# Who copies the last state of four scans: VectorE or GpSimd

## The chip, the cores and the metric

One core of one Trainium2 chip runs the whole program in one launch. The metric is device time in microseconds (us), the median of several runs. Five engines have their own instruction streams and meet only through semaphores: TensorE (PE, with its weight loads as PEld), VectorE (DVE), ScalarE (ACT), GpSimd (POOL) and SyncE (SP), which here only issues transfers.

## The reference, cut to what matters

The program is a chain of four layers on x of shape (2, 4096, 512). The first, a state-space (Mamba) layer, is where the change lies:

```python
proj = x @ in_proj_w                     # hidden and gate, 1024 channels each
hs = silu(causal_conv4(hidden) + conv_b)
dt, Bm, Cm = split(hs @ x_proj_w)        # 128, 16, 16; each rms-normed
dt = softplus(dt @ dt_proj_w + dt_proj_b)
dA  = exp(dt[..., None] * A)             # A: 1024 x 16
dBu = (dt * u)[..., None] * Bm[:, :, None, :]
s = dA_t * s + dBu_t                     # the scan over time, for each channel and each of 16 states
y = sum_n s_n * C_n                      # C of this time step
out = ((y + u * D) * silu(gate)) @ out_proj_w
```

Three further layers (a mixed linear layer, a linear attention, a spline layer) follow in another function of the program, which the change does not touch.

## The kernel before

`mamba_block` works in 16 periods: 8 chunks of 512 time steps for each of 2 sequences, the two in turn (`periods`). A period has U = 32 units, numbered k. A unit is one group of 128 channels with 4 of the 16 states. What happens to unit k:

- PE, `b_product(k)` (L737): dt·u times B for the four states into the PSUM tile BU. There is one BU, so it waits until the four scans of unit k-1 are done (`scan_done`).
- ACT (L501): exp(dt·A) into the slot s[k % 4], four instructions.
- DVE (L651): four scans of 512 steps over s[k % 4] and BU, in place in s, each started from a column of `state`. Each adds one to `scan_done`.
- DVE, `piece(k)`: a share of the work for the next period or the previous output, placed by hand: `Y_AT`, `HID_AT`, `RES_AT`, `MIN_AT`, `MAX_AT`, `DTU_AT` and single numbers say which unit carries what. Units 14 to 21 carry one convolution each (L536, L540, three L544 with drains between). Unit 19 has `dt_floor` (L574) directly behind the third L544. Unit 3 has `add_res` (L590) and `dt_max` (L579). Unit 4 has `ln_apply` (two L528) and, directly behind, `dt_times_u` (L584). Units 13, 22 and 30 have L579 and then L584, which waits for it. Unit 10 has statistics (L518 to L523, with drains) and `add_res`, unit 11 `ln_apply` and `add_res`, unit 27 `ssm_norm` (L562, two L566), units 1, 9 and 25 `y_out` (L600, reads PSUM), units 0, 12 and 29 `dt_floor`. Units 5, 7, 8, 23, 24, 28 and 31 carry nothing.
- DVE (L656): a tensor_reduce over an axis of length 1, that is a copy, of the last column of the four scans into `state[:, b, k, :]` (128x4), where the scans of the same sequence's next chunk start. It adds one to `state_saved`.
- POOL (L335): waits for `state_saved`, then multiplies s by C (the tile Cb) in place, in two instructions of 128x1024. It must come behind the copy, since it overwrites the column. Each adds one to `z_ready`.
- PE, `y_sum` (L754): sums the products of a pair of units into PSUM; at an even k it needs the first half of unit k-1. It then frees the slot for ACT (`sum_done`).

POOL also has three small powers a period (L300, L304), each ahead of the product of units 2, 10 and 26, and four products of 128x512 (L310), behind the products of units 28, 29, 30 and 0. `dve.sem_inc` is an instruction of its own; in `add_res` one stands behind a wait for the result of L590 (L593, L594). PE's order in a unit is: wait for the scans of unit k-1, `b_product(k)`, and then `y_sum` and projections in an order fixed by k.

The inner part of the DVE body and of the POOL body, and all that calls them:

Of the kernel before, what the change touches and what calls it, by code (L numbers as in the profile page):

```python
# [9 lines left out]
ALU = mybir.AluOpType  # L10
ACT = mybir.ActivationFunctionType
AX = mybir.AxisListType

P = 128
T = 512
# [6 lines left out]
def wait(eng, sem, value):  # L22

    if not isinstance(value, int) or value > 0:
        eng.wait_ge(sem, value)
# [33 lines left out]
def mamba_block(nc, x, in_w, chan, xproj_w, dt_w, out_w, eye, tokmask, x1):  # L59
# [9 lines left out]
    U = G * NQ  # L69
# [4 lines left out]
    SLOTS = 4  # L74
# [6 lines left out]
    with ctx:  # L81
        def sb(name, shape, dt=F32):
            return ctx.enter_context(nc.sbuf_tensor(name, shape, dt))
# [4 lines left out]
        def sem(name):  # L88
            return ctx.enter_context(nc.semaphore(name))
# [7 lines left out]
        skip_w = sb("skip_w", [P, G, 64])  # L97
        mask = sb("mask", [P, 32])
        minus_half = sb("minus_half", [P, NT * 3])
        xt = sb("xt", [P, 2, HID])  # L100
        dts = sb("dts", [P, 2, T])
        xnT = sb("xnT", [P, KB, T])
# [8 lines left out]
        s = [sb(f"s{i}", [P, 4, T]) for i in range(SLOTS)]  # L111
        Cb = [sb(f"Cb{i}", [P, 4 * T]) for i in range(2)]
        state = sb("state", [P, BATCH, U, 4])
# [29 lines left out]
        spread_ready = sem("spread_ready")  # L143
        dbu_ready, da_ready, scan_done, state_saved = (
            sem("dbu_ready"), sem("da_ready"), sem("scan_done"), sem("state_saved"))
        z_ready, sum_done, y_ready = sem("z_ready"), sem("sum_done"), sem("y_ready")
        res_loaded = [sem(f"res_loaded{i}") for i in range(2)]
        x1_ready = sem("x1_ready")
# [44 lines left out]
        def periods(eng, body):  # L193

            for b in range(BATCH):
                body(0, b, b, b == 0, False)
            with eng.Fori(1, NI - 1) as i:
                for b in range(BATCH):
                    body(i, b, i * BATCH + b, False, False)
            for b in range(BATCH):  # L200
                body(NI - 1, b, (NI - 1) * BATCH + b, False, b == BATCH - 1)
# [89 lines left out]
        @block.gpsimd  # L291
        def _(pool):
            nc.gpsimd.memset(minus_half[:], -0.5)
            nc.gpsimd.memset(state[:], 0.0)
            nc.gpsimd.memset(hist[:], 0.0)
            pool.drain().then_inc(consts_ready, 1)

            def ln_power(c_next, half):
                wait(pool, stats_ready, 2 * c_next + half + 1)
                nc.gpsimd.tensor_tensor(rstd[:], ve[:], minus_half[:, 0:2], ALU.pow).then_inc(rstd_ready, 1)  # L300

            def ssm_power(c_next):
                wait(pool, ssq_ready, c_next + 1)
                nc.gpsimd.tensor_tensor(rssm.rearrange("p j n -> p (j n)"), ssq.rearrange("p j n -> p (j n)"),  # L304
                                        minus_half[:], ALU.pow).then_inc(rssm_ready, 1)

            def spread_b(c_next, nq):
                pool.wait_ge(ssm_ready, c_next + 1)
                lo = RANK + 4 * nq
                nc.gpsimd.tensor_tensor(spread[:, nq], mask[:].unsqueeze(1).unsqueeze(3).to_broadcast([P, TB, 32, 4]),  # L310
                                        ssm[:, :, lo:lo + 4].unsqueeze(2).to_broadcast([P, TB, 32, 4]),
                                        ALU.mult).then_inc(spread_ready, 1)

            ln_power(0, 0)
            ln_power(0, 1)
            ssm_power(0)
            pool.wait_ge(small_loaded, 48)
            for nq in range(NQ):
                spread_b(0, nq)

            def body(i, b, c, first, last):
                for k in range(U):
                    if k == 2 and not last:
                        ln_power(c + 1, 0)
                    if k == 10 and not last:
                        ln_power(c + 1, 1)
                    if k == K_SUMS and not last:
                        ssm_power(c + 1)
                    q = k // 2
                    if k % 2 == 0:  # L330
                        wait(pool, c_loaded[q % 2], 16 * (c * (U // 4) + (q % (U // 2)) // 2 + 1))
                    wait(pool, state_saved, c * U + k + 1)
                    for part in range(2):
                        pair = s[k % SLOTS][:, 2 * part:2 * part + 2, :].rearrange("p n t -> p (n t)")
                        nc.gpsimd.tensor_tensor(pair, pair, Cb[q % 2][:, 2 * part * T:2 * part * T + 2 * T],  # L335
                                                ALU.mult).then_inc(z_ready, 1)
                    if k == 0 and not first:
                        wait(pool, dbu_ready, c * U)
                        spread_b(c, 3)
                    if k in (28, 29, 30) and not last:  # L340
                        nq = k - 28
                        wait(pool, dbu_ready, c * U + 26 + 2 * nq)
                        spread_b(c + 1, nq)

            periods(pool, body)

        @block.scalar
# [166 lines left out]
        def _(dve):  # L514
# [10 lines left out]
            def ln_apply(c_next, half):  # L525
                wait(dve, rstd_ready, 2 * c_next + half + 1)
                for j in range(2):
                    last_ = nc.vector.tensor_scalar(xt[:, j, :], xt[:, j, :], mv[:, j, 0:1], rstd[:, j:j + 1],  # L528
                                                    ALU.subtract, ALU.mult)
                last_.then_inc(xn_ready, 1)  # L530
# [65 lines left out]
            def y_out(p, c, slot):  # L596
                wait(dve, gate_ready, 2 * c + p // 2 + 1)
                dve.wait_ge(sum_done, c * U + UP * (p + 1))
                for r in range(2):
                    nc.vector.tensor_tensor(u[slot][:, 2 * p + r, :], Y[r][:], gate[:, 2 * p + r, :], ALU.mult  # L600
                                            ).then_inc(y_ready, 1)
# [13 lines left out]
            def body(i, b, c, first, last):  # L615
                def piece(k):

                    if k == 1 and not first:
                        y_out(3, c - 1, 1 - b)
                    if k in Y_AT:  # L620
                        y_out(Y_AT[k], c, b)
                    if not last:
                        if k in (2, 10):
                            ln_stats(c + 1, 0 if k == 2 else 1)
                        if k in (4, 11):
                            ln_apply(c + 1, 0 if k == 4 else 1)
                        if k - 1 in HID_AT:
                            conv(steady, HID_AT[k - 1], c, 1 - b, 1 - b)
                        if k == K_SUMS:
                            ssm_sums(c + 1)  # L630
                        if k == K_NORM:
                            ssm_norm(steady, c, c + 1)
                    if k in RES_AT:
                        if first:
                            dve.drain().then_inc(steady.taken["dve"], 1)
                        else:
                            add_res(steady, RES_AT[k], c, c - 1)
                    if k in MIN_AT and not (last and MIN_AT[k] == 0):
                        dt_floor(steady, MIN_AT[k], c)
                    if k in MAX_AT and not (last and MAX_AT[k] == 0):  # L640
                        p = MAX_AT[k]
                        dt_max(p, PAIRS * c + (p if p else PAIRS))
                    if k in DTU_AT and not (last and DTU_AT[k] == 0):
                        p = DTU_AT[k]
                        dt_times_u(p, PAIRS * c + (p if p else PAIRS), c if p else c + 1, b if p else 1 - b)

                for k in range(U):
                    wait(dve, dbu_ready, c * U + k + 1)
                    for n in range(4):
                        wait(dve, da_ready, 4 * (c * U + k) + n + 1)  # L650
                        nc.vector.tensor_tensor_scan(s[k % SLOTS][:, n, :], s[k % SLOTS][:, n, :], BU[:, n::4],  # L651
                                                     state[:, b, k, n:n + 1], ALU.mult, ALU.add
                                                     ).then_inc(scan_done, 1)
                    piece(k)
                    wait(dve, scan_done, 4 * (c * U + k + 1))
                    nc.vector.tensor_reduce(state[:, b, k, :], s[k % SLOTS][:, :, T - 1:T], AX.X, ALU.max  # L656
                                            ).then_inc(state_saved, 1)

            periods(dve, body)
            y_out(3, NCH - 1, 1)  # L660
# [1139 lines left out]
```

## Time and the profile before

| what | value |
|---|---|
| median of 3 runs | 5924.46 us (5921.22 to 5928.32) |
| profiled execution, its time | 5923.98 us |
| profiled execution, its span | 5922.2 us |
| state-space layer, first to last L656 | 128.4 to 3790.5 us |
| busy in the span | PE 86%, DVE 83%, POOL 55%, PEld 51%, ACT 44% |

### The profile page before, as it was taken

To read this page: it belongs to the slowest core of one execution; us is meant where nothing else is said; L and a number is where in the kernel's file an instruction comes from. 1 tells how busy PE (TensorE), PEld (TensorE's weight loads), DVE (VectorE), ACT (ScalarE), POOL (GpSimd) and SP (SyncE) were. 2 spreads that over 40 slices of the span, in tenths; PEclk is the share of its full clock that TensorE was granted. 3 is DMA by queue.
4 is the path that set the end of the run, shared out by engine and by line. 5 is a ranking of instruction groups with operands and counts; after the bars stand their busy time and mean duration, and the time that the engine had idled before them with its cause. 6 is when DMAs were issued, how large, how long until landed. Compare 5 with 4: busy or idle time off the path is not lost. (4 is left out here: it accounts for less than half of the span.)

```text
span 5922.2 us, 110904 instructions
## 1 busy us (share of the span) xinstructions
PE 5088.3 (86%) x41157; PEld 3047.7 (51%) x41157; DVE 4925.7 (83%) x7468; ACT 2610.0 (44%) x4180; POOL 3231.1 (55%) x1675
## 2 busy tenths in 40 slices
PE   6899999999999999999999998668888888888822
PEld 3444444444444444444444444246666777777722
DVE  3888988888888889889888888568888888888888
ACT  3655655655556556556556555212222222222200
POOL 1676676676766766766766767423333333333323
PEclk9999999999999999999999999879999998899855
DMA  2221222222222222212222222220000000000034
GB/s 84 76 101 65 100 99 74 94 87 79 101 81 85 101 79 86 95 72 101 90 76 101 85 81 94 91 86 25 20 22 22 20 23 20 24 20 20 18 111 138
DMA packets 139954, 421.27 MB, mean 71 GB/s; under 512 B 38368, under 2 KB 39904, under 8 KB 106592
## 3 DMA queue, kind: packets, MB, share of 16 engines
q1 hardware_dynamic: 136672, 411.75, 19.8%
q8 instruction: 268, 4.39, 0.3%
q10 hardware_dynamic: 2816, 3.51, 0.2%
q14 instruction: 198, 1.62, 0.1%
HBM read 361.99 MB, written 53.22 MB: 70 GB/s over the span
## 5 line engine op out<-in xcount | busy, mean ns | idle before, releaser
L335 POOL TENSOR_TENSOR s<-s,Cb 128x1024 f32<-128x1024 f32 x1024 | 2393.7, 2359 | 1083.8 <-DVE state L656 1073.0
L651 DVE TENSOR_TENSOR_SCAN s<-s,state,BU 128x512 f32<-128x512 f32 x2048 | 2452.7, 1260 | 425.4 <-PE BU L737 391.5
L501 ACT ACTIVATE s<-dt,ch 128x512 f32<-128x512 f32 x2048 | 1305.6, 712 | 778.6 <-PE Y L754 777.1
L754 PE MATMUL Y<-s,ident 64*64 64x512 f32 x8192 | 1011.8, 609 | 76.2 <-POOL s L335 75.3
L683 PE MATMUL PJ<-xnT,w_in 128*128 128x512 f32 x2048 | 946.9, 606 | 9.1 <-ACT dtuT L367 5.7
L737 PEld LDWEIGHTS BU<-spread,dtuT 32*128 32x128 f32 x16384 | 512.7, 189 | 528.4 <-DVE s L651 403.0
L737 PE MATMUL BU<-spread,dtuT 32*128 32x128 f32 x16384 | 611.2, 286 | 145.5 <-DVE s L651 140.8
L683 PEld LDWEIGHTS PJ<-xnT,w_in 128*128 128x128 f32 x2048 | 370.1, 190 | 479.0 <-issue 424.2
L754 PEld LDWEIGHTS Y<-s,ident 64*64 64x64 f32 x8192 | 279.3, 134 | 571.5 <-issue 533.8
L728 PE MATMUL PJ<-w_out,u 128*128 128x512 f32 x1024 | 472.8, 606 | 8.2 <-ACT xnT L371 6.7
L1110 POOL TENSOR_TENSOR x1t<-x1t,bias_b 128x512 f32<-128x512 f32 x64 | 81.1, 1267 | 525.8 <-DVE xa L1282 525.8
L1463 PE MATMUL bank<-w_high_o,aTs 128*128 128x512 f32 x512 | 214.2, 485 | 125.7 <-DVEq L1385 125.7
L728 PEld LDWEIGHTS PJ<-w_out,u 128*128 128x128 f32 x1024 | 185.1, 190 | 243.3 <-issue 225.9
L544 DVE SCALAR_TENSOR_TENSOR u<-hid,ch,u 128x512 f32<-128x512 f32 x384 | 287.5, 749 | 19.1
L1104 POOL TENSOR_TENSOR r_t<-x,x3n 128x512 f32<-128x512 f32 x64 | 82.6, 1290 | 344.8 <-DVE x3n L1282 344.8
L694 PE MATMUL PJ<-w_xp,u 128*128 128x160 f32 x1024 | 253.0, 404 | 9.6 <-issue 6.5
L694 PEld LDWEIGHTS PJ<-w_xp,u 128*128 128x128 f32 x1024 | 243.1, 329 | 27.2 <-issue 20.8
L1463 PE MATMUL bank<-w_high_f,xaT 128*128 128x512 f32 x512 | 198.7, 452 | 12.5 <-DVE xaT L1287 12.5
L1225 ACT ACTIVATE junk<-bank 128x512 f32<-128x512 f32 x64 | 38.2, 598 | 380.4 <-PE bank L1535 380.4
L1463 PEld LDWEIGHTS bank<-w_high_o,aTs 128*128 128x128 f32 x512 | 119.8, 234 | 163.8 <-issue 135.2
L1161 ACT COPY qk_all<-bank 128x512 f32<-128x512 f32 x128 | 75.1, 587 | 227.1 <-PE bank L1463 227.1
L367 ACT COPY dtuT<-PJ 128x512 f32<-128x512 f32 x128 | 68.8, 587 | 231.3 <-PE PJ L723 231.3
(218 smaller groups left out, 7634.8 us busy)
## 6 DMA issues: line engine op xcount, KB each, us to landing
Cb<-bc SPq DMA_DIRECT2D x256, 1024.0 KB, 4.9
res<-in_x SPq DMA_DIRECT2D x64, 256.0 KB, 4.9
x<-res SPq DMA_DIRECT2D x64, 256.0 KB, 5.2
x1t<-x SPq DMA_DIRECT2D x64, 256.0 KB, 2.6
out<-r_t SPq DMA_DIRECT2D x64, 256.0 KB, 2.0
xt<-in_x SPq DMA_DIRECT2D x31, 512.0 KB, 5.5
x_all<-out SPq DMA_DIRECT2D x16, 512.0 KB, 4.2
scm<-out SPq DMA_DIRECT2D x16, 512.0 KB, 4.6
```

Source lines behind the costliest of these rows:

```text
L335: nc.gpsimd.tensor_tensor(pair, pair, Cb[q % 2][:, 2 * part * T:2 * part * T + 2 * T], ALU.mult).then_inc(z_ready, 1)
L501: nc.scalar.activation(s[k % SLOTS][:, n, :], dt[p % 2][:, gi, :], ACT.Exp, scale=ch[:, 2 * p + gi, 7 + 4 * nq + n:8 + 4 * nq + n]).then_i ...
L544: last_ = nc.vector.scalar_tensor_tensor(out, h_[:, tap:tap + T], ch[:, m, tap:tap + 1], out, ALU.mult, ALU.add)
L651: nc.vector.tensor_tensor_scan(s[k % SLOTS][:, n, :], s[k % SLOTS][:, n, :], BU[:, n::4], state[:, b, k, n:n + 1], ALU.mult, ALU.add).then ...
L683: last_ = nc.tensor.matmul(bank[:], w_in[:, kb, lo:lo + P], xnT[:, kb, :], start=(kb == 0), stop=(kb == KB - 1))
L694: last_ = nc.tensor.matmul(bank[:, tb % 2 * SP_:(tb % 2 + 1) * SP_], by_block(u[slot][:, g, :])[:, tb], w_xp[:, g, :], start=(g == 0), sto ...
L728: last_ = nc.tensor.matmul(bank[:], u[slot][:, g, j * P:(j + 1) * P], w_out[:, g, :], start=(g == 0), stop=(g == G - 1))
L737: last_ = nc.tensor.matmul(BU[:, i * T:(i + 1) * T].rearrange("p (t b n) -> p b t n", b=TB, n=4)[:, tb], dtuT[rows, gi, tb, :], spread[row ...
L754: last_ = nc.tensor.matmul(Y[r][y_rows(r, gi), :], ident[rows, rows], s[(k_even + gi) % SLOTS][rows, n, :], start=False, stop=(n == 3 and ...
L1104: nc.gpsimd.tensor_tensor(r_t[s_][:], x3[s_][:], x3n[s_][:], ALU.add).then_inc(S["r_ready"], 1)
L1110: nc.gpsimd.tensor_tensor(x1t[s_][:], x1t[s_][:], bias_b[:], ALU.add).then_inc(S["x1b_ready"], 1)
L1463: last_ = nc.tensor.matmul(b_[:], src[part][:, k, :], wt, start=(k == 0 and i == 0), stop=(k == KB - 1 and i == 2))
```

## The change

The copy leaves DVE. POOL waits for the four scans itself, multiplies the last column by a tile of ones into `state`, then waits for `pieces_done` and for its own copy, and multiplies by C. DVE's stream gets a bare `sem_inc(pieces_done)` behind the piece in place of the wait and the copy.

```diff
+        ones4 = sb("ones4", [P, 4])
...
+        pieces_done = sem("pieces_done")
...
             nc.gpsimd.memset(minus_half[:], -0.5)
+            nc.gpsimd.memset(ones4[:], 1.0)
...
                     if k % 2 == 0:
                         wait(pool, c_loaded[q % 2], 16 * (c * (U // 4) + (q % (U // 2)) // 2 + 1))
+                    pool.wait_ge(scan_done, 4 * (c * U + k + 1))
+                    last_col = s[k % SLOTS][:, :, T - 1]
+                    nc.gpsimd.tensor_tensor(state[:, b, k, :], last_col, ones4[:], ALU.mult).then_inc(state_saved, 1)
+                    wait(pool, pieces_done, c * U + k + 1)
                     wait(pool, state_saved, c * U + k + 1)
...
                     piece(k)
-                    wait(dve, scan_done, 4 * (c * U + k + 1))
-                    nc.vector.tensor_reduce(state[:, b, k, :], s[k % SLOTS][:, :, T - 1:T], AX.X, ALU.max
-                                            ).then_inc(state_saved, 1)
+                    dve.sem_inc(pieces_done, 1)
```

## Rows read from the trace of the kernel before

**Rows 1.** The page, section 2: busy tenths of PE in 40 slices, and DVE.

```profile
PE   6899999999999999999999998668888888888822
DVE  3888988888888889889888888568888888888888
```

**Rows 2.** Waits: who waited for whom, us in total, times, longest.

```profile
POOL s L335 <- DVE state L656: 1073.0, 462, 32.2
```

**Rows 3.** Timeline of DVE, units 3 to 6 of one period: start, duration, instructions, idle before.

```profile
1992.73 1.52 DVE L579 TENSOR_TENSOR dt<-dt,dts 128x1024 f32<-128x1024 f32 x1 [0.23 <-DVE res L590]
...
1998.95 0.97 DVE L528 TENSOR_SCALAR xt<-xt,mv,rstd 128x512 f32<-128x512 f32 x2
1999.84 1.21 DVE L584 TENSOR_TENSOR dts<-dt,u 128x1024 f32<-128x1024 f32 x1
2000.98 0.14 DVE L656 TENSOR_REDUCE state<-s 128x4 f32<-128x4 f32 x1
2001.05 4.78 DVE L651 TENSOR_TENSOR_SCAN s<-s,state,BU 128x512 f32<-128x512 f32 x4
2005.86 0.16 DVE L656 TENSOR_REDUCE state<-s 128x4 f32<-128x4 f32 x1
2007.21 1.28 DVE L651 TENSOR_TENSOR_SCAN s<-s,state,BU 128x512 f32<-128x512 f32 x1 [1.19 <-PE BU L737]
```

**Rows 4.** Timeline of POOL, the second product of unit 2.

```profile
1990.82 2.35 POOL L335 TENSOR_TENSOR s<-s,Cb 128x1024 f32<-128x1024 f32 x1
```

**Rows 5.** Timeline of PE, b_product of unit 6.

```profile
2005.88 1.17 PE L737 MATMUL BU<-spread,dtuT 32*128 32x128 f32 x32
```

**Rows 6.** Timeline of DVE, the end of unit 19 and the scans of 20.

```profile
1874.88 2.39 DVE L544 SCALAR_TENSOR_TENSOR u<-hid,ch,u 128x512 f32<-128x512 f32 x3
1877.19 0.69 DVE L574 TENSOR_SCALAR dts<-dt 128x1024 f32<-128x1024 f32 x1
1877.79 0.15 DVE L656 TENSOR_REDUCE state<-s 128x4 f32<-128x4 f32 x1
1877.86 4.78 DVE L651 TENSOR_TENSOR_SCAN s<-s,state,BU 128x512 f32<-128x512 f32 x4
```

**Rows 7.** The copy by source line, all 512: duration ns min/median/max, first and last start.

```profile
L656 DVE TENSOR_REDUCE state<-s x512: 141/153/163, 128.4 to 3790.5; 128x4 f32<-128x4 f32 x171
```

**Rows 8.** DVE's sequencer by source line, units 4 and 19.

```profile
L583 DVEq EVENT_SEMAPHORE  x1: 21/21/21, 1994.3 to 1994.3; - x1
L573 DVEq ALU_OP  x1: 40/40/40, 1876.5 to 1876.5; - x1
```

**Rows 9.** By source line, last layer, 5806 to 5812 us.

```profile
L1647 DVE TENSOR_TENSOR qk_all<-vv,kTs x2: 417/2582/4747, 5806.3 to 5806.6; 128x256 f32<-128x256 f32 x2
L1619 POOL TENSOR_TENSOR x_all<-x_all,decay x1: 4543/4543/4543, 5806.5 to 5806.5; 128x2048 f32<-128x2048 f32 x1
```

**Rows 10.** y_out by source line, all 128: PSUM and one SBUF input.

```profile
L600 DVE TENSOR_TENSOR u<-Y,gate x128: 659/674/692, 186.7 to 3800.0; 128x512 f32<-128x512 f32 x128
```

**Rows 11.** POOL by line and form: count, busy us, mean ns of one, idle before.

```profile
L335 POOL TENSOR_TENSOR s<-s,Cb 128x1024 f32<-128x1024 f32 x1024 | 2393.7, 2359 | 1083.8 <-DVE state L656 1073.0 <-DMA Cb<-bc 10.1
L1104 POOL TENSOR_TENSOR r_t<-x,x3n 128x512 f32<-128x512 f32 x64 | 82.6, 1290 | 344.8 <-DVE x3n L1282 344.8
L300 POOL TENSOR_TENSOR rstd<-ve,minus_half 128x2 f32<-128x2 f32 x32 | 22.3, 697 | 103.6 <-DVE ve L523 103.6
```

**Rows 12.** Timelines of unit 11's end: DVE, POOL, and PE's y_sum of unit 12.

```profile
2047.97 0.16 DVE L656 TENSOR_REDUCE state<-s 128x4 f32<-128x4 f32 x1 [0.24 <-DVE res L590]
2048.17 4.79 DVE L651 TENSOR_TENSOR_SCAN s<-s,state,BU 128x512 f32<-128x512 f32 x4
2048.21 4.69 POOL L335 TENSOR_TENSOR s<-s,Cb 128x1024 f32<-128x1024 f32 x2 [2.06 <-DVE state L656]
2050.72 1.95 PE L754 MATMUL Y<-s,ident 64*64 64x512 f32 x16 [1.12 <-POOL s L335]
```

**Rows 13.** Timelines of unit 27: DVE, and POOL's products of unit 26.

```profile
1937.13 1.26 DVE L562 TENSOR_TENSOR xt<-xt 128x512 f32<-128x512 f32 x1
1938.32 0.35 DVE L566 TENSOR_TENSOR xt<-xt 128x64 f32<-128x64 f32 x2
1939.03 4.79 DVE L651 TENSOR_TENSOR_SCAN s<-s,state,BU 128x512 f32<-128x512 f32 x4 [0.30 <-PE BU L737]
...
1933.17 4.67 POOL L335 TENSOR_TENSOR s<-s,Cb 128x1024 f32<-128x1024 f32 x2
```

## The prediction

> **What bounds the kernel now.** I read the page first: PE and DVE share the state-space layer about evenly, both at 8 or 9 tenths in nearly every slice [rows 1], so the order of work decides, and shares of busy time do not. Then the waits: POOL's longest, 1073 us, is for the copy that the change removes [rows 2], over two microseconds a unit. It looks like a prize, but POOL has that time to spare: it works 4.7 us in a unit of about 7.2. So I went to the timelines of DVE, POOL and PE over one whole period (the scans of unit 0 start 230 to 231 us apart) and noted in each unit what the scans waited for. There are two kinds of unit. With a short piece, the next scans wait for BU: scan, b_product, scan; the copy at 2005.86 lies wholly inside the 1.19 us that DVE waits [rows 3, 5]. With a long piece (units 3, 4, 10, 11, 13 to 22, 30) DVE runs without a gap from scan over piece and copy to the next scan; there what DVE does is on the path. In between PE alone is on it (units 23 to 27, and most of 31, 0, 1, 2, 6 to 9, 12).
>
> **What the change gives.** The copy lasts 0.153 us [rows 7], but the next scan starts 0.07 us after it starts, since neighbours overlap [rows 3, 6]. So its removal gives DVE 0.07 us, not 0.15, where DVE is on the path: units 13 to 21 (9 x 0.07 = 0.63 us) and units 3 and 4 (0.14). Behind `add_res` in units 10 and 11 the copy starts on an empty datapath and the scan follows 0.20 us later [rows 12]; a semaphore instruction still stands there, so I take 0.15 us for unit 10. The end of unit 11 is the one place where POOL's start is on the path: the product starts 0.08 us after the copy's end at 2048.13, PE waits 1.12 us for its first half, and b_product(13) comes right behind that work [rows 12]. `pieces_done` comes about when the copy started, so the product gains 0.15 us, of which I give back 0.05 for POOL's copy slipping between the two L528 of that unit. Sum: 0.63 + 0.14 + 0.15 + 0.10 = 1.02 us a period, in 15 of 16 periods (the last prepares no next one), 15.3 us. In all other units the copy is covered by the wait for b_product or by PE.
>
> **What the change costs on POOL.** The trace has no 4-element multiplication on POOL. From 1290 ns for 512 and 2359 ns for 1024 columns [rows 11], a column costs 2.09 ns, which leaves 0.22 us for an instruction with next to no work. The other end is the 0.70 us of the power of two columns [rows 11], dear by its power. I take 0.22, as it is the same operation, and about 0.08 more for POOL to wait for its own result, as the product now starts that long after the copy [rows 12]. In units without a piece the product then starts 0.1 to 0.2 us later than now. PE asks for it late there: the first halves of units 5, 7 and 23 are ready over 2 us before its y_sum. POOL itself is idle 2 us a unit. So this is hidden. At 0.70 us the copy would reach into the first L544 of seven convolution units, by some 0.27 us each (it would end 0.40 after L544's start, of which 0.13 is start-up), 1.9 us a period, 28 us: that goes into the range.
>
> **What it costs on DVE: who is let in.** This is the term that I think decides. Two facts of the trace:
>
> First, DVE and POOL shut each other out. In the last layer the second of two back-to-back L1647 takes 4747 ns instead of 417, because a POOL instruction of 4543 ns, issued at 5806.5 while the first ran, was let in between the two [rows 9]. The same holds here: L579 took 1.52 us at 1992.73 because L335 ran until 1993.17; it ended 1.08 us after that [rows 3, 4]. Instructions with one input in PSUM, the scans and L600, do not suffer (L600: 692 ns at most [rows 10]). The Trainium skill ("SBUF — State Buffer", section on the two separate sides) states it as a lock: DVE instructions with two SBUF inputs, or in a mode that uses two ports, and GpSimd instructions take a shared port pair for the whole instruction, and the other side blocks fully. The trace agrees, with the 4747 ns; by the rule the sum would be the one below, and by the titles of the engines alone (they run in parallel) it would be the 15.3 us gained.
>
> Second, DVE's sequencer runs ahead. Unit 4's wait in front of L584 passed at 1994.3, when unit 4's scans had just begun and L584 was 5.5 us away; unit 19's arithmetic in front of L574 was done at 1876.5, 0.7 us before L574 started [rows 8, 3, 6]. A bare `sem_inc` behind these instructions is thus done when they are issued, not when they have ended. Before, the product waited for the copy, which ran behind the piece; the copy kept POOL out of it. Now `pieces_done` does not. Unit by unit:
>
> *Unit 4.* Scans end at 1999.02, L528 twice and L584 follow back to back. `pieces_done` has long been given. POOL's copy asks at 1999.1, gets in behind the first L528 (1999.46) and is done by about 1999.6; the product asks 0.08 us later, during the second L528, and is let in when that ends, at 1999.92. Its first instruction then holds L584 off for 2.25 us (2.36, less the start that it has behind it), to 2002.17; L584 ends 1.08 us after that, as L579 did, at 2003.25 instead of 2001.05: 2.2 us. b_product(6) started at 2005.88 right when the scans were done [rows 5], so all of it counts. The second instruction comes behind L584 and meets only scans.
>
> *Unit 19.* The third L544 runs 1876.52 to 1877.27, L574 next [rows 6]. `pieces_done` comes at about 1876.7, the product asks before 1877.0, is let in at 1877.27, and holds L574 until 1879.52; it ends some 0.4 to 0.5 us later, near 1879.98, instead of 1877.88: 2.1 us, in the middle of the stretch where DVE has no gap.
>
> *Elsewhere* nothing that needs the ports stands behind another such instruction with `pieces_done` already given: convolution units give it during the last L544; units 13, 22 and 30 after L579 has ended, since L584 waits for it; `add_res` and the statistics hold it back by a wait or a drain; y_out reads PSUM. Unit 27 is open, see below.
>
> **Sum.** Per period 2.2 + 2.1 - 1.02 = 3.3 us, times 15: 49 us. Against the profiled execution's 5923.98 us (0.5 under the median) that is 5973 us, 0.8% slower. The three layers behind are unchanged.
>
> **The rivals.**
>
> *A third stall, in unit 27.* L562 and two L566 of 64 columns follow each other, `pieces_done` given early. POOL's product of unit 26 already holds L562 until 1937.84, 1.26 us instead of some 0.7 [rows 13]; it will end 0.3 later, behind the new copy. Then the copy gets in behind L562, and the product of 27 asks 0.08 us after the copy, while the first L566 needs about as long: a tie. If POOL wins, the second L566 waits 2.25 us and scan 28, which had 0.30 us of waiting, starts that much later (PE's transpose of this result as well). 15 x 2.25 = 34 us more: 6007 us.
>
> *Only one of the two stalls*, because the other's request comes a little too late or L528 does not need the ports: about 5941 us.
>
> *None: the faster side.* If `sem_inc` waits for DVE's datapath, or a back-to-back DVE run is not interrupted, only the gains stay: 5924.0 - 15.3 = 5909 us, 0.26% faster. For it: the first product never now starts during a piece, so this kernel's trace has no such meeting. Against it: rows 9, where the run was interrupted, and rows 8. It decides where the product starts after the last piece instruction in units 4 and 19.
>
> *More stalls*, as both instructions of a product getting in, or a dear copy in the convolution units: 6020 us and above.
>
> *The change does nothing*, as copy and semaphore cancel: only by chance between the cases.
>
> **Chances.** Two stalls 0.45, three 0.24, one 0.10, none 0.13, more 0.08. The forecast is the likeliest, 5973 us; its own range, from 2.0 to 2.4 us a stall and 0.5 to 1.3 us of gain, is 5960 to 5984. The range for 8 in 10 takes in one and three stalls: 5936 to 6012. A measurement of this kernel can tell 0.2%, 12 us, from no change. Slower 0.85: two, three, more and 0.08 of the one-stall case; same 0.03: the other 0.02 of that and 0.01 of none, should the gains be smaller; faster 0.12.
>
> **What would show it.** In the profile after: 512 POOL instructions 128x4 of 0.2 to 0.3 us. L584 four a period, of which one in 15 periods near 3.4 us (now 1.2); L574 one near 2.8 (now 0.7). L335 starting during L528 and L544, so with a longer mean than 2359 ns. Conv units shorter by 0.07 us; period up from 230.5 to about 234. L566 up to 2.5 us if unit 27 stalls as well. Wrong would be: L335 never starting before the piece ends; L584 and L574 unchanged; or the copy near 0.7 us, with L544 up from 0.75.

## The result and the profile after

The changed kernel takes 5937.62 us (median of 20 runs, 5926.39 to 5950.81), the kernel before 5922.58 (20 runs, 5918.55 to 5928.32): ratio 1.0026, 95% interval 1.0019 to 1.0033. It is slower, just inside the range of 5936 to 6012 and on the side forecast, but by 15 us and not by 49. Its runs also spread over 24 us, the kernel before's over 10, so a difference of a few us between single profiled executions of two kernels says little.

The profiled execution has a span of 5939.7 us. The first thing to look at is where the state-space layer ends, and for that the first instruction of the next function serves (a memset on POOL, by source line: duration, first and last start). Before:

```profile
L1089 POOL MEMSET ones<- x1: 204/204/204, 3831.8 to 3831.8; 128x128 f32 x1
```

After:

```profile
L1094 POOL MEMSET ones<- x1: 205/205/205, 3873.6 to 3873.6; 128x128 f32 x1
```

The layer became 41.8 us longer. The three layers behind went from 5922.2 - 3831.8 = 2090.4 us to 5939.7 - 3873.6 = 2066.1 us, 24.3 us shorter, though no line of them was changed. So there are two things to explain.

**The first layer.** The copy on POOL and the two lines that were to stall, by source line:

```profile
L337 POOL TENSOR_TENSOR state<-s,ones x512: 188/199/1276, 126.2 to 3832.0; 128x4 f32<-128x4 f32 x171
L581 DVE TENSOR_SCALAR dts<-dt x64: 665/670/2864, 97.2 to 3753.6; 128x1024 f32<-128x1024 f32 x64
L591 DVE TENSOR_TENSOR dts<-dt,u x64: 1195/1226/3382, 101.5 to 3774.0; 128x1024 f32<-128x1024 f32 x64
```

The copy costs 0.20 us on an idle POOL; the longer ones are held up by DVE. L581 (`dt_floor`, was L574) reaches 2.86 us, L591 (`dt_times_u`, was L584) 3.38 us. Going through the trace instruction by instruction, L581 is held up in unit 19 of all 15 periods, L591 in unit 4 in 8 of the 15, and L573 (unit 27, was L566; 219 ns at most) never. Unit 19 [rows 6], timelines of DVE and of POOL:

```profile
2128.02 2.40 DVE L551 SCALAR_TENSOR_TENSOR u<-hid,ch,u 128x512 f32<-128x512 f32 x3
2130.33 2.85 DVE L581 TENSOR_SCALAR dts<-dt 128x1024 f32<-128x1024 f32 x1
2133.11 1.27 DVE L658 TENSOR_TENSOR_SCAN s<-s,state,BU 128x512 f32<-128x512 f32 x1
...
2129.90 5.52 POOL L342 TENSOR_TENSOR s<-s,Cb 128x1024 f32<-128x1024 f32 x2 [1.88 <-DVEq L662]
```

The product is released by the bare increment (L662) and starts at 2129.90, while the last L551 still runs (to 2130.42). L581 then takes 2.85 us instead of 0.69: it waits for the first half of the product. From the first L551 to the next scan it now takes 5.09 us; before it was 2.98 [rows 6]. That is the 2.1 us of the prediction.

Unit 4 [rows 3] in a period with the stall:

```profile
2019.06 3.37 DVE L591 TENSOR_TENSOR dts<-dt,u 128x1024 f32<-128x1024 f32 x1
...
2013.74 4.66 POOL L342 TENSOR_TENSOR s<-s,Cb 128x1024 f32<-128x1024 f32 x2
2018.35 0.39 POOL L337 TENSOR_TENSOR state<-s,ones 128x4 f32<-128x4 f32 x1
2018.88 5.77 POOL L342 TENSOR_TENSOR s<-s,Cb 128x1024 f32<-128x1024 f32 x2
```

and in one without:

```profile
2490.09 1.22 DVE L591 TENSOR_TENSOR dts<-dt,u 128x1024 f32<-128x1024 f32 x1
...
2489.36 0.41 POOL L337 TENSOR_TENSOR state<-s,ones 128x4 f32<-128x4 f32 x1 [0.25 <-DVE s L658]
2489.92 3.61 POOL L342 TENSOR_TENSOR s<-s,Cb 128x1024 f32<-128x1024 f32 x1
```

In both the product is issued 0.17 to 0.18 us before L591. Once it gets in first, once L591 does and the product is held up (3.61 us instead of 2.36). What differs is further back: in the first the product of unit 3 still ran (2013.74 + 4.66 = 2018.40) when the scans of unit 4 ended (2018.24), and the copy queued behind it; in the second POOL had been idle for 0.25 us.

Where unit 4 stalls there is more: PE then waits about 2 us (6 in the first period) ahead of b_product(6), which it does in no period without the stall, and in six of the eight its granted clock falls to half for 3.4 us about there. In the period shown the mean granted clock is 0.73 of full speed from 2027.20 to 2033.60 us, and b_product takes 1.78 us and the projection 4.72, against 1.17 and 3.70 in the neighbouring units:

```profile
2027.19 1.78 PE L742 MATMUL BU<-spread,dtuT 32*128 32x128 f32 x32 [2.21 <-DVE s L658]
2028.90 4.72 PE L733 MATMUL PJ<-w_out,u 128*128 128x512 f32 x8
```

**The layers behind.** The waits of DVE between 4000 and 5750 us, before:

```profile
DVE xaT L1287 <- issue: 38.2, 12, 3.4
```

In the profile after, that line is gone, and with it two smaller ones (L1322 and L1318, 14 waits each, 10.9 us together); no DVE wait put down to "issue" is longer than 0.5 us there. "Issue" is time in which an engine waited for nothing that the profile shows. The queue that brings instructions says what it was. Before, then after:

```profile
q14 instruction: 198, 1.62, 0.1%
```

```profile
q14 instruction: 130, 1.06, 0.1%
```

Before, 59 of its packets fall between 4200 and 5500 us, in the middle of the loop of the later layers: five in each pass of 109 us, which is four steps. After, there are none. This loop has 353 instructions on DVE in both kernels (as many as the trace of before has from 4500.0 to 4609.1 us), but in the changed one it lies 64 instructions lower, since DVE's part of the first layer became shorter: ahead of the memset the trace has 7066 DVE records instead of 7450, 64 fewer in each of the six passes of the first layer's loop.

### The profile page after: what moved, and what is told of

It reads as the page before. It is cut to its first block and busy times, and to the rows that moved or that the text cites. A ratio compares the mean times of both kernels' runs of the same rounds, so it can differ in the third digit from the quotient of the medians.

```text
span 5939.7 us, 111545 instructions
## 1 busy us (share of the span) xinstructions
PE 5084.9 (86%) x41157; PEld 3038.5 (51%) x41157; DVE 4931.6 (83%) x6956; ACT 2609.4 (44%) x4180; POOL 3546.1 (60%) x2188
## 5 line engine op out<-in xcount | busy, mean ns | idle before, releaser
L342 POOL TENSOR_TENSOR s<-s,Cb 128x1024 f32<-128x1024 f32 x1024 | 2529.1, 2491 | 314.9 <-DVEq L662 271.1
L337 POOL TENSOR_TENSOR state<-s,ones 128x4 f32<-128x4 f32 x512 | 183.9, 359 | 459.7 <-DVE s L658 447.1
L551 DVE SCALAR_TENSOR_TENSOR u<-hid,ch,u 128x512 f32<-128x512 f32 x384 | 287.6, 749 | 19.0
L1230 ACT ACTIVATE junk<-bank 128x512 f32<-128x512 f32 x64 | 38.2, 598 | 380.3 <-PE bank L1540 380.3
```

The costliest lines, as they stand in the source:

```text
L337: nc.gpsimd.tensor_tensor(state[:, b, k, :], last_col, ones4[:], ALU.mult).then_inc(state_saved, 1)
L551: last_ = nc.vector.scalar_tensor_tensor(out, h_[:, tap:tap + T], ch[:, m, tap:tap + 1], out, ALU.mult, ALU.add)
```

## The experiments

Where a run only names units, the edit is to the changed kernel. "Layer" is the start of the next function's memset, as above.

**A drain in units 4 and 19.**

```diff
-                    dve.sem_inc(pieces_done, 1)
+                    if k in (4, 19):
+                        dve.drain().then_inc(pieces_done, 1)
+                    else:
+                        dve.sem_inc(pieces_done, 1)
```

> The changed kernel, but in units 4 and 19 pieces_done is given by a drain, that is after the piece has ended, and by a bare semaphore instruction elsewhere. Theory A (POOL's product is let in between two DVE instructions in units 4 and 19): L581 and L591 never over 1.3 us there; the state-space layer ends some 58 us earlier than in the changed kernel (which ended it at 3873.6, the kernel before at 3831.8), near 3815 us, so 16 us ahead of the kernel before. Theory B (the loss is the copy on POOL, its 0.2 to 0.4 us and the later start of the product): the layer still ends at 3870 us or later, as the copy is unchanged and drains are added. The whole time follows the layer's end, give or take 24 us for the layers behind, whose time differed by that between the two profiles.

Measured: 5892.44 us, ratio to the kernel before 0.9951 (0.9938 to 0.9965). Layer 3824.0 us, 49.6 us earlier than in the changed kernel. The two lines have no long instance left:

```profile
L581 DVE TENSOR_SCALAR dts<-dt x64: 661/669/699, 98.7 to 3702.6; 128x1024 f32<-128x1024 f32 x64
L591 DVE TENSOR_TENSOR dts<-dt,u x64: 1201/1226/1229, 103.0 to 3723.3; 128x1024 f32<-128x1024 f32 x64
```

Theory A holds, B falls. The layer is 9 us later than I expected: the drain gives back about 0.3 us a period in each of the two units, which last 0.31 and 0.28 us longer than in the kernel before.

**VectorE copies in units 4 and 19, GpSimd elsewhere.**

```diff
+                    if k in (4, 19):
+                        wait(dve, scan_done, 4 * (c * U + k + 1))
+                        nc.vector.tensor_reduce(state[:, b, k, :], s[k % SLOTS][:, :, T - 1:T], AX.X, ALU.max
+                                                ).then_inc(saved_dve, 1)
+                    else:
+                        dve.sem_inc(pieces_done, 1)
```

> The changed kernel, but in units 4 and 19 alone VectorE makes the copy behind its piece, as before the change, and the product waits for it. Theory A: no stall at L581 and L591; the layer ends within 3 us of the run with two drains, near 3817 us, and the whole time is 5900 to 5912 us if the layers behind take 2090 us as in the kernel before. Theory B: 28 of 30 copies a period are still POOL's, so the layer ends near 3870 us.

Measured: 5888.04 us, ratio 0.9941 (0.9927 to 0.9954), the fastest of all; no stall, layer 3819.6, 12.2 us ahead of the kernel before. The whole is below the expected 5900 to 5912 because the layers behind take 2067.6 us here too. (POOL makes 30 of the 32 copies of a period here, not 28 of 30.)

**The drain in unit 19 alone, and in unit 4 alone.**

> A drain in front of pieces_done in unit 19 alone. Theory A: the 15 stalls of 2.1 us at L581 go, 31 us; those at L591 in unit 4 stay in about half of the periods; the layer ends near 3842 us. Theory B: no change from 3874.

> A drain in front of pieces_done in unit 4 alone. Theory A: all 15 stalls at L581 stay, none at L591; each of the 8 periods that had one was 3.4 us longer than the 7 others, so 27 us go and the layer ends near 3847 us. If unit 4's stall costs only its own 2.1 us, 17 us go and it ends near 3857. Theory B: no change from 3874.

Measured: unit 19 alone 5911.08 us, ratio 0.9984 (0.9974 to 0.9993), layer 3842.5, with 8 stalls at L591 left; by this the 15 stalls cost 31.1 us, 2.07 each. Unit 4 alone 5918.55 us, ratio 0.9994 (0.9985 to 1.0004), layer 3850.0, with 15 stalls at L581 left; by this the 8 stalls cost 23.6 us, 2.95 each, more than the 2.1 us that the instruction itself is late. Both prices rest on one profiled execution of each kernel, and the drain's own cost is taken off. Counted from the run with both drains, the same stalls cost 26.0 us (3850.0 - 3824.0) and 18.5 (3842.5 - 3824.0); by the medians of all runs, 26.5 and 19.1. So a stall costs 1.7 to 2.1 us in unit 19 and 2.3 to 3.0 in unit 4.

**Nothing holds the product back.**

```diff
-                    wait(pool, pieces_done, c * U + k + 1)
```

> The changed kernel without POOL's wait for pieces_done, so that nothing holds the product back but the scans and its own copy. Theory A: in the eight convolution units the two instructions of the product are let in between the three L551, at the drains, and hold two of them up by about 2.2 us each, some 4.4 us a unit; 8 units and 15 periods give up to 530 us, so 6300 to 6500 us. L586 to L591 in units 13, 22 and 30 suffer likewise. Theory B: the start of the product is not what costs: 5940 us or a little less.

Measured: one run, 6374.5 us. The product now starts 0.3 us behind the scans. A convolution unit, DVE and POOL:

```profile
2104.70 6.28 DVE L550 SCALAR_TENSOR_TENSOR u<-hid,ch,u 128x512 f32<-128x512 f32 x3
...
2104.77 5.66 POOL L341 TENSOR_TENSOR s<-s,Cb 128x1024 f32<-128x1024 f32 x2
```

Three L550 take 6.28 us instead of 2.39: the two halves of the product and the three instructions of DVE let each other in by turns. So `pieces_done` is what makes the moved copy bearable, and where it comes too early, in unit 19 and in some periods in unit 4, the same happens once.

**Filler instructions, to move VectorE's code.** At the end of DVE's part of the first layer, in the kernel before (128, then 64) and in the changed one (64):

```diff
                 add_res(after, j, 0, NCH - 1)
+            for _ in range(64):
+                dve.sem_inc(filler, 1)
```

> The kernel before, with 128 bare semaphore instructions at the end of VectorE's part of the state-space layer, 21 ns each. Theory C (the layers behind run 24 us shorter in the changed kernel because VectorE's program lies 64 instructions lower there and its loop of 353 instructions is no longer fetched anew in every pass): the stalls of DVE at L1287 put down to issue, 12 of 3.2 us, go; the layers behind take 2066 us instead of 2090, and the whole takes 5899 to 5902 us. Theory D (those 24 us come from where the TensorE clock's low stretches fall, moved by the longer first layer): 2.7 us more shift hardly anything; the layers behind stay at 2090 us with their 12 stalls, the whole at 5922 to 5926 us.

> The changed kernel with 64 such instructions at the same place, which puts VectorE's later loops where they were before the change. Theory C: the 12 stalls of 3.2 us come back, the layers behind take 2090 us, the whole some 24 us more than the changed kernel's 5937.6, near 5962 us. Theory D: 1.3 us more, 5939 us.

> The kernel before with 64 semaphore instructions at the end of VectorE's part of the first layer. 128 of them left the 12 stalls of DVE put down to issue, and 64 brought them back in the changed kernel; the instruction queue's packets are 8192 bytes. Theory C, with a period of 128 instructions: 64 move the loop to where it lies in the changed kernel; the 12 stalls of 3.2 us go, the layers behind take 2066 us, and the whole takes some 5 us (the 64 instructions) less 24: 5902 to 5906 us. Theory E (the changed kernel's later layers are shorter for a cause other than place): 2090 us, 12 stalls, 5928 us.

| kernel | fillers | layer | layers behind | DVE xaT waits put down to issue | whole |
|---|---|---|---|---|---|
| before | 0 | 3831.8 | 2090.4 | 12, 38.2 us | 5922.6 |
| before | 128 | 3841.6 | 2089.7 | 12, 37.7 us | 5933.3, ratio 1.0018 (1.0009 to 1.0027) |
| before | 64 | 3837.9 | 2066.9 | none | 5904.9, ratio 0.9963 (0.9949 to 0.9976) |
| changed | 0 | 3873.6 | 2066.1 | none | 5937.6 |
| changed | 64 | 3872.3 | 2088.8 | 13, 41.2 us | 5962.8, ratio 1.0065 (1.0051 to 1.0078) |

In the kernel before the layer ends 6 and 10 us later with the fillers: more than their 21 ns each (1.3 and 2.7 us), and what the rest is was not looked into. The run with 128 fillers missed: I had taken 256 instructions as the period, from the Trainium skill ("Advanced Engine Details and Errata", section ISA Cache: lines of 256 instructions, two of them). The runs say otherwise: 64 instructions switch the stalls on or off, 128 change nothing. The other two runs came out within 1 us of the number or inside the range expected. Theory D falls: where the first layer ends does not decide, since 64 fillers make it 6 us later in the kernel before and take 23.5 us off the layers behind. In the twelve profiles these take 2089 to 2090 us in the three that have the stalls and 2059 to 2068 in the nine that have not. The clock goes along: it is granted at half for 645 to 656 us of the layers behind in those three and for 596 to 616 in the nine, so part of the 24 us may be the clock's.

**One more instruction on POOL in unit 4.**

```diff
+                    if k == 4:
+                        nc.gpsimd.tensor_tensor(spare[:], ones4[:], ones4[:], ALU.mult)
                     wait(pool, pieces_done, c * U + k + 1)
```

> The changed kernel, but in unit 4 POOL does one more multiplication of 128x4, of no use, between its copy and the product, so the product asks about 0.15 to 0.25 us later. If unit 4 is a race between the product and L591 lost or won by a few ns: L591 always wins, no L591 over 1.3 us, 15 stalls at L581 as before, and the first layer ends near the 3850 us of the run with the drain in unit 4; the whole time 5914 to 5920 us. If another thing decides in unit 4, 8 of 15 stalls stay.

Measured: 5936.05 us, ratio 1.0025 (1.0016 to 1.0034), layer 3866.9, 7 stalls at L591. The extra multiplication (L340) in POOL's timeline, in a period without and in one with the stall:

```profile
2017.25 1.64 POOL L340 TENSOR_TENSOR spare<-ones 128x4 f32<-128x4 f32 x1
...
2248.65 0.20 POOL L340 TENSOR_TENSOR spare<-ones 128x4 f32<-128x4 f32 x1
```

The edit did not do what it was made for. In the 7 periods with the stall the multiplication fits into the time in which the product waited for the copy anyway, and the product starts 0.64 to 0.65 us behind the scans, as in the changed kernel (0.64 to 0.66): it asks no later. In the other 8 the multiplication itself is held up until DVE's L594 (the changed kernel's L591) has ended. So whether a slightly later request would have lost is not tested. The run does show that the two kinds of period differ already right behind the copy, 0.2 us before the product asks.

**A drain in unit 3.**

```diff
+                    if k == 3:
+                        dve.drain().then_inc(pieces_done, 1)
+                    else:
+                        dve.sem_inc(pieces_done, 1)
```

> The changed kernel with a drain in front of pieces_done in unit 3. In the traces so far L591 is held up in unit 4 exactly in those periods in which the product of unit 3 started after L586 and so still ran when the scans of unit 4 ended. With the drain it starts after L586 in every period. Theory F (that order decides): 15 of 15 stalls at L591, and the first layer ends some 7 x 3.4 = 24 us later than in the changed kernel, near 3897 us; the whole near 5961 us. Theory G (a lottery of a few ns): 5 to 10 stalls, 3870 to 3880 us, 5938 us.

Measured: 5918.40 us, ratio 0.9991 (0.9982 to 1.0001), layer 3852.2, and not 15 stalls at L591 but none. Both theories missed. The trace says why the order was the wrong condition: the product of unit 3 now starts 0.13 to 0.20 us behind the end of L586 in all 15 periods, but the drain also makes the scans of unit 4 start some 0.3 us later, so that this product ends 0.12 to 0.30 us before they end. Another condition fits all that was seen: in 75 periods of five traces (the changed kernel, unit 19 drained, 64 fillers, the extra multiplication, unit 3 drained) L591 is held up in all 30 in which the product of unit 3 still ran when the scans of unit 4 ended, and in none of the other 45.

## Why the prediction was right and wrong

*Two engines shut each other out, and `pieces_done` comes too early*: right, and it decided the sign. Shown by the two drains, and at large by the run without the wait.

*Unit 19, 2.1 us in every period*: right. The unit lasts 10.15 us on average and 8.07 in the kernel before; 15 of 15 periods stall.

*Unit 4, 2.2 us in every period*: wrong in the count. I took it as certain that the product is let in behind the second L535. It asks at the same time in every period, but gets in only when the copy had queued behind the product of unit 3. That in turn hangs on unit 3: when the product of unit 2 (which in the period shown waited for Cb) still runs at the issue of L586, as in these 8 periods and in none of the other 7, the product of unit 3 starts 0.2 us after L586 instead of during it. So 8 stalls and not 15. Their price was off the other way: 2.3 to 3.0 us. In the changed kernel unit 4 lasts 2.17 us longer with the stall than without, and unit 6, where PE has waited and runs at half clock, 0.96; unit 3 is 0.69 us longer in the same periods, which goes with the stall but is not caused by it. 18.5 to 23.6 us in all, against the 33 forecast.

*Unit 27, given 0.24*: did not happen; no instance of L573 is long, and L569 (was L562) waits at most 0.34 us longer for the product of unit 26.

*Gain where the copy was on DVE's path, 15.3 us*: 12.2 us by the mixed kernel, which keeps the gain in 30 of 32 units; right in kind. Units 12 to 22 are mostly 0.06 to 0.24 us shorter there, but unit 3 is 0.44 us longer, which the sum did not have.

*The copy on POOL, 0.22 us, hidden*: right (0.20). The dear copy of the range, with 0.13 us of "start-up" that no row shows, did not come up. The forecast's own range was also added up wrongly: its bounds give 5964 to 5988 us, not 5960 to 5984; nothing hangs on it.

The first layer thus came out 41.8 us longer where 49 were forecast: fewer stalls in unit 4, at a higher price each, and a smaller gain. *The failed step is the last sentence of the sum, "The three layers behind are unchanged".* Their work is, but their place in VectorE's program is not, and 24.3 us came back: VectorE's loop there lost 12 waits of 3.2 us. With that place restored (64 fillers) the changed kernel takes 5962.8 us, 40 us over the kernel before, near the forecast. The trace of before showed the price openly, as 12 waits of DVE for "issue" at one line, and I did not ask what those were. That the time still fell inside the range, close to the 5941 us of the rival with only one stall, is luck: both units stalled.

Open: why a copy queued behind a running product lets POOL in before L591 and one on an idle POOL does not, with the same times in the records to some 0.02 us; that the loop is fetched anew because of its place is inferred from the packets, the waits and the five rows of the table, not seen directly; and why 38 us of such waits, 49 with the two smaller ones, cost 24 (other engines' waits seem to cover the rest; this was not tried).

## What to carry to other kernels

A semaphore instruction behind a VectorE instruction says that it was issued, not that it has ended. If POOL starts a long instruction on it, that can land between two VectorE instructions and hold the second for its whole length; wherever two such instructions stand back to back, let a drain or a copy on VectorE behind them give the signal (both tried here), or the last instruction itself (not tried). And before believing a difference of half a per cent, compare the parts of the program that were not changed: a loop that is refetched in every pass can be switched on or off by an edit in front of it, and a wait put down to "issue" at one line, once a pass, is its mark.

## What the runs showed of the hardware

- A loop of 353 VectorE instructions is refetched or not by its place: 64 instructions further and the 12 stalls of 3.2 us come or go, 128 and they stay. It costs 24 us here, 0.4% of the whole: more than the 15 us between the two kernels.
- After a wait of 2.2 us PE's granted clock fell from 2.4 to 1.2 GHz for 3.4 us, and b_product and the projection behind it took 6.50 us instead of 4.87. Of the seven waits of 1.9 to 2.2 us at this place in the changed kernel six went with such a fall.
- Moving the copy in 30 of 32 units is worth 0.6% with the code in its lucky place (5888.0), but of these 35 us 12.2 are the move (the layer) and 22.8 the place (the layers behind): the kernel before with 64 fillers reaches 5904.9 without the move.
